# A two-layer convolution and low-rank kernel on one core: order and queues of the moved sample columns

## The reference, cut to what matters

```python
# layer 0: a grouped convolution over the 1024 columns, with a row of context per sample
h = conv1d(x, weight, groups=4, taps=9, pad=4) + ctx[:, :, None] + bias[None, :, None]
# then a dense layer 1024 -> 1024 with a rank-masked low-rank term (the rank chosen per row)
x = x + h @ W.T + b + sel(h @ A[:r].T @ B[:, :r].T)
# layer 1: a per-sample 64x64 channel mixture (weights from a small network), then a dense layer
# 1024 -> 1024 with a sparsemax-weighted mixture of 8 rank-16 experts
h = agg_w @ x + agg_b
x = x + h @ W_base.T + b_base + experts(h)
```

## Time and profile before

| | us |
|---|---|
| median of 3 runs | 519.87 |
| lowest, highest | 519.02, 521.14 |
| the profiled execution's own time | 518.63 |
| its span | 516.8 |
| PE busy | 497.5 (96%) |
| DVE busy | 364.4 (71%) |
| ACT busy | 152.4 (29%) |
| POOL busy | 167.9 (32%) |
| mean granted TensorE clock | 0.993 |

### The profile page before, as it was taken

One profiled execution on the slowest core, in us unless ns is written; L12 is line 12 of the kernel. 1 busy time (PEld: TensorE's weight loads), 2 busy tenths in 40 slices (PEclk: granted clock), 3 DMA queues, 4 the chain that ended last, 5 costly groups with the idle time before them and its releaser, 6 DMA issues.

```text
span 516.8 us, 8425 instructions
## 1 busy us (share of the span) xinstructions
PE 497.5 (96%) x2857; PEld 456.8 (88%) x2857; DVE 364.4 (71%) x797; ACT 152.4 (29%) x322; POOL 167.9 (32%) x140
## 2 busy tenths in 40 slices
PE   9999999999989989798898999999999999999997
PEld 8989999999879879688797988899898989989886
DVE  3956997567765877687669976775676857566654
ACT  4732335152424236133235312211211212121200
POOL 1000020042455256445604316161523416161530
PEclk9999999999989989999999999999999999999999
DMA  8844206348565764856899924241424233160312
GB/s 319 302 157 153 81 1 185 112 134 268 199 217 192 249 202 127 275 176 190 280 376 413 412 101 150 98 167 44 174 90 146 99 122 124 62 204 1 122 42 82
DMA packets 46182, 88.47 MB, mean 171 GB/s; under 512 B 4795, under 2 KB 21787, under 8 KB 46140
## 3 DMA queue, kind: packets, MB, share of 16 engines
q1 hardware_dynamic: 37084, 65.56, 38.3%
q10 hardware_dynamic: 9056, 22.38, 11.4%
HBM read 58.79 MB, written 24.97 MB: 162 GB/s over the span
## 4 chain that ended last, share of the span: by engine, by line
PE 62%; DVE 9%; POOL 9%; DMA 7%; issue 7%; SPq 5%; ACT 1%; DVEq 0%; POOLq 0%
PE b_p L1725 5%; DMA z_moved<-a_lo_place 5%; PE b_x L1745 4%; PE b_x L1744 4%; PE b_x L1742 4%; PE b_m L1673 3%; PE b_p L1726 3%; PE b_y L1745 3%; PE b_y L1742 3%; PE b_y L1744 3%; DMA wp_place<-in_wcat 2%; POOL mixed L645 2%; PE b_m L1701 2%; SPq L432 2%; DVE a_lo L1140 2%
## 5 line engine op out<-in xcount | busy, mean ns | idle before, releaser
L1725 PE MATMUL b_p<-wp,a_hi 128*128 128x464 f32 (+1 forms) x224 | 76.5, 391 | 8.6 <-DVE a_lo L1140 8.4
L722 ACT CAST a_hi<-mixed 128x512 fp32r<-128x512 f32 x63 | 37.7, 620 | 148.8 <-DVE mixed L1107 80.3
L654 POOL TENSOR_TENSOR xs<-xs,mixw_sb 128x512 f32<-128x512 f32 x28 | 38.6, 1390 | 122.9 <-DMA xs<-x_scratch 87.8
L1140 DVE TENSOR_TENSOR a_lo<-mixed,a_hi 128x512 fp32r<-128x512 f32 x63 | 54.5, 898 | 20.5 <-ACT a_hi L722 20.0
L1726 PE MATMUL b_p<-wp,a_lo 128*128 128x232 f32 (+1 forms) x224 | 61.5, 275 | 0.0
L1725 PEld LDWEIGHTS b_p<-wp,a_hi 128*128 128x128 f32 x224 | 43.6, 195 | 15.5 <-issue 9.4
L733 ACT CAST s_hi<-s_sums 128x512 fp32r<-128x512 f32 x56 | 34.7, 621 | 72.5 <-POOL s_sums L617 34.6
L1148 DVE TENSOR_TENSOR s_lo<-s_sums,s_hi 128x512 fp32r<-128x512 f32 x56 | 46.5, 881 | 7.6 <-POOL s_sums L622 7.4
L1301 DVE TENSOR_TENSOR xs<-b_x,xs 128x464 f32<-128x464 f32 (+2 forms) x52 | 33.3, 640 | 25.4 <-PE b_x L1785 15.6
L1742 PE MATMUL b_y<-wb_hi,s_hi 128*128 128x464 f32 (+2 forms) x112 | 42.2, 377 | 3.8 <-ACT a_lo_place L849 2.0
L1726 PEld LDWEIGHTS b_p<-wp,a_lo 128*128 128x128 f32 x224 | 44.4, 198 | 0.6
(11 more groups left out here) (308 smaller groups left out, 1313.3 us busy)
## 6 DMA issues: line engine op xcount, KB each, us to landing
blk<-x_scratch SPq DMA_DIRECT2D x16, 512.0 KB, 4.0
xs<-in_x SPq DMA_DIRECT2D x30, 256.0 KB, 3.3
x_scratch<-xs SPq DMA_DIRECT2D x30, 256.0 KB, 4.1
xs<-x_scratch SPq DMA_DIRECT2D x28, 256.0 KB, 3.0
out_dram<-xs SPq DMA_DIRECT2D x27, 256.0 KB, 2.2
w_raw<-in_wcat SPq DMA_DIRECT2D x8, 546.0 KB, 8.9
blk<-in_xwhole SPq DMA_DIRECT2D x8, 512.0 KB, 4.2
praw<-in_wcat ACTq DMA_DIRECT2D x8, 464.0 KB, 4.3
```

The lines of the kernel that those rows point to most:

```text
L654: pool.tensor_tensor(x_rows, x_rows, bbase[:, a:b], ALU.add).then_inc(x_biased[q], 1)
L722: act.copy(a_hi[:, op, :, :], mixed[:, op, :, :]).then_inc(ahi_done[op], 1)
L1140: dve.tensor_tensor(a_lo[:, op, :, :], mixed[:, op, :, :], hi(a_hi[:, op, :, :]), ALU.subtract).then_inc(alo_done[op], 1)
L1725: pe.matmul(both, x_hi, wp[:, k, :, 0:PLAIN[l]], start=(k == 0), stop=False, skip_group_check=True)
```

## The change

Six things are moved, no arithmetic is changed. `move_z` is split: SyncE keeps two of its four DMAs (one of 112 rows, one of 15), ScalarE issues the other two, right behind the `take_z` of the sample. SyncE moves (a,1) before the x and block loads and (b,1) before tile b+2's block load; its x loads of pair 7 come later, with two waits. GpSimd adds (a,0) and (a,1) before `prep`, (b,0) and (b,1) behind it. ScalarE loads the weight piece after the second `cast_x`, takes and moves (b,1) before any `prep_split`, and stores the piece after A22. VectorE's list is reordered: `prep_split` and `low_x` of the next pair's first tile come later, the results that free banks between them.

```diff
--- before.py
+++ after.py
@@ -428,9 +428,7 @@
                 if sample(T, n) > 1:
                     sp.wait_ge(z_added, sample(T, n) - 1)
                 sp.dma_start(dst[1:EDGE + 1, 0, :], src[0:EDGE, 1, :]).then_inc(z_landed[n], 16)
-                sp.dma_start(dst[0:EDGE, 1, :], src[1:EDGE + 1, 0, :]).then_inc(z_landed[n], 16)
                 sp.dma_start(dst[EDGE + 1:P, 0, :], src[EDGE:P - 1, 1, :]).then_inc(z_landed[n], 16)
-                sp.dma_start(dst[EDGE:P - 1, 1, :], src[EDGE + 1:P, 0, :]).then_inc(z_landed[n], 16)
 
             half = FR_TAPS + HALF_FRONT
             sp.dma_start(first_in[:, FR_TAPS:half], front[:, FR_TAPS:half]).then_inc(s_taps[0], 16)
@@ -506,20 +504,18 @@
                     sp.wait_ge(fin12, g)
                     store_x(1, g - 1)
                     move_z(a, 0)
+                    move_z(a, 1)
                     stored(3, g - 1)
                     stored(1, g - 1)
                     load_x(3, g)
                     load_x(1, g)
                     sp.wait_ge(mix_done, steps(a + 1))
                     load_blocks(a + 2)
-                    move_z(a, 1)
                     move_z(b, 0)
+                    move_z(b, 1)
                     sp.wait_ge(mix_done, steps(b + 1))
                     load_blocks(b + 2)
-                    move_z(b, 1)
                     if g == PAIRS - 2:
-                        load_x(3, g + 1)
-                        load_x(1, g + 1)
                         sp.wait_ge(agg_stored, 16)
                     load_agg(g + 2)
                     sp.wait_ge(sum_done, steps(b + 1))
@@ -527,6 +523,11 @@
                     sp.wait_ge(fin11, g + 1)
                     sp.wait_ge(finq[0], g + 1)
                     store_x(0, g)
+                    if g == PAIRS - 2:
+                        sp.wait_ge(took_u2, made(g))
+                        sp.wait_ge(took_p5, made(g))
+                        load_x(3, g + 1)
+                        load_x(1, g + 1)
                     sp.wait_ge(fin21, g + 1)
                     sp.wait_ge(finq[1], g + 1)
                     store_x(2, g)
@@ -666,12 +667,14 @@
             pool.wait_ge(aggb_stored, 16)
             pool.memset(z_moved[1][:, :, :], 0.0).then_inc(zeroed, 1)
             for g in range(FULL, LAST + 1):
+                if shifted(2 * g + 2):
+                    add_z(2 * g + 2, 0)
+                    add_z(2 * g + 2, 1)
                 if PREP_FIRST <= g <= PREP_LAST:
                     prep(g)
                 if shifted(2 * g + 2):
-                    for T in (2 * g + 2, 2 * g + 3):
-                        for n in range(2):
-                            add_z(T, n)
+                    add_z(2 * g + 3, 0)
+                    add_z(2 * g + 3, 1)
                 if g == PAIRS:
                     pool.wait_ge(s_bbase, 16)
                     pool.wait_ge(gated, 4 * (2 * g + 2))
@@ -848,39 +851,51 @@
                 dst = z_out[n].rearrange("p v (a c) -> p v a c", c=CH)[:, :, :, CH // 2 * gp:CH // 2 * (gp + 1)]
                 act.copy(dst, src).then_inc(z_taken, 1)
 
+            def move_z(T, n):
+
+                src, dst = z_out[n], z_moved[n]
+                act.wait_ge(z_taken, 2 * sample(T, n) + 2)
+                if sample(T, n) == 0:
+                    act.wait_ge(zeroed, 3)
+                if sample(T, n) > 1:
+                    act.wait_ge(z_added, sample(T, n) - 1)
+                act.dma_start(dst[0:EDGE, 1, :], src[1:EDGE + 1, 0, :]).then_inc(z_landed[n], 16)
+                act.dma_start(dst[EDGE:P - 1, 1, :], src[EDGE + 1:P, 0, :]).then_inc(z_landed[n], 16)
+
             def shift_pair(g):
 
                 a, b = 2 * g + 2, 2 * g + 3
                 split_s(S2, g)
                 split_s(S4, g)
-                prep_load(g)
                 take_z(a, 0, 0)
                 take_z(a, 0, 1)
+                move_z(a, 0)
                 cast_x(b, 0)
                 gate_exp(2 * g)
                 gate_exp(2 * g + 1)
                 take_z(a, 1, 0)
                 take_z(a, 1, 1)
+                move_z(a, 1)
                 cast_x(b, 1)
+                prep_load(g)
                 take_z(b, 0, 0)
                 take_z(b, 0, 1)
-                prep_split(0, g)
-                prep_split(1, g)
+                move_z(b, 0)
                 split_ut(2 * g)
                 split_ut(2 * g + 1)
+                split_a(A11, g + 1)
+                take_z(b, 1, 0)
+                take_z(b, 1, 1)
+                move_z(b, 1)
+                split_a(A12, g + 1)
+                for part in (0, 1, 3, 2):
+                    prep_split(part, g)
                 if shifted(a + 2):
                     cast_x(a + 2, 0)
-                take_z(b, 1, 0)
-                take_z(b, 1, 1)
-                prep_split(3, g)
-                prep_split(2, g)
-                split_a(A11, g + 1)
-                split_a(A12, g + 1)
-                if shifted(a + 2):
                     cast_x(a + 2, 1)
-                prep_store(g)
                 split_a(A21, g + 1)
                 split_a(A22, g + 1)
+                prep_store(g)
                 split_s(S1, g + 1)
                 split_s(S3, g + 1)
                 if g == PREP_LAST:
@@ -1494,30 +1509,31 @@
                 sum_shift(b, 0, 1)
                 split_ut(2 * g)
                 split_ut(2 * g + 1)
-                if shifted(a + 2):
-                    low_x(a + 2, 0)
                 sum_shift(b, 1, 0)
                 sum_shift(b, 1, 1)
-                for part in (0, 1, 3, 2):
-                    prep_split(part, g)
-                dve.wait_ge(p_done[P6], made(g))
-                take(b_x, 1, g, took_u2)
                 split_a(A11, g + 1)
-                split_a(A12, g + 1)
                 dve.wait_ge(c11_done, g + 1)
                 dve.wait_ge(took_p1, made(g))
                 take(b_z, 0, g, fin11, BANK)
+                split_a(A12, g + 1)
+                dve.wait_ge(p_done[P6], made(g))
+                take(b_x, 1, g, took_u2)
+                prep_split(0, g)
+                prep_split(1, g)
                 dve.wait_ge(p_done[P5], made(g))
                 take(b_y, 3, g, took_p5)
+                dve.wait_ge(c21_done, g + 1)
+                take(b_w, 2, g, took_w, BANK)
+                prep_split(3, g)
+                prep_split(2, g)
                 dve.wait_ge(fin11, g + 1)
                 take_plain(0, g)
-                dve.wait_ge(c21_done, g + 1)
-                take(b_w, 2, g, took_w, BANK)
-                if shifted(a + 2):
-                    low_x(a + 2, 1)
                 dve.wait_ge(p_done[P7], made(g))
                 dve.wait_ge(took_w, made(g))
                 take(b_x, 2, g, fin21)
+                if shifted(a + 2):
+                    low_x(a + 2, 0)
+                    low_x(a + 2, 1)
                 take_plain(1, g)
                 split_a(A21, g + 1)
                 split_a(A22, g + 1)
```

## The result

| | before | changed |
|---|---|---|
| median, us | 520.28 (4 runs beside it) | 534.06 (4 runs) |
| lowest to highest, us | 519.02 to 521.14 | 533.29 to 535.36 |
| span of the profiled execution, us | 516.8 | 531.9 |
| mean granted TensorE clock | 0.993 | 0.987 |

The changed kernel is slower: ratio 1.0278, 95% interval 1.0241 to 1.0315. The forecast of 516.9 us, its range and its sign were wrong.

A forecast was written before the change was run, and what follows sets the result against it. The VectorE-ScalarE ring was taken to stay the bound: terms summed from 34.84 to 33.8 us a turn, -4.2 us over four turns, 3 after pair 7, giving 516.9 us; 8-in-10 range 508.5 to 523.5.

The forecast's parts named there:

- -4.09: VectorE's idle time before the last splits, waiting for sample (b,1), goes: 4.09 us less per turn.
- -1.1: Two prep casts leave ScalarE's list before the low-rank casts, for which VectorE idles: 1.1 us less per turn.
- -0.86: low_x of the next pair no longer makes VectorE wait for its block: 0.86 us less per turn.
- -0.7: VectorE's s_lo shrinks as GpSimd's sums come earlier, low_x moves beside them: 0.7 us less per turn (0 to -1.3).
- issues on ScalarE: ScalarE's two DMA issues per sample block its next cast: +1.46, +1.2, +1.46, +1.3 us behind the four samples.
- the later load: Weight piece issued some 10 us later, landing 4.3 us after; VectorE's first prep_split needs its sums: +0.3 us (0 to 1.5).
- The wait for (b,1): Second plain part: PE's largest wait, 8.4 us in four pieces, comes from the late sample (b,1) and leaves.
- the ring: VectorE and ScalarE hand each other work; one turn, 34.84 us, was to become 33.8 and stay the bound.
- gave back 1.2: Pair 7: ScalarE stands some 2.7 us for the store before load_home, cutting the gain from 4.2 to 3 us.
- B: Rival: ScalarE's issues are hidden and cost nothing, PE is the bound; 11 us less, 509 us; chance 0.22.
- C: Rival: slower, two of ScalarE's small issues per pair take 1.8 us under backlog; 524.5 us; chance 0.18.
- D: Rival: no change, pair 7's load takes all the gain or issues are 0.3 us longer each; 519.5 us; chance 0.20.

The follow-up runs named there:

- e5_sync_early: Changed kernel with all four DMAs of a sample on SyncE and the weight piece loaded before the first take: 511.81 us.
- e1_load_early: Changed kernel with one thing undone, ScalarE loading the weight piece before the first take again: 525.25 us.
- e2_sync_all: Changed kernel with all four DMAs of a sample issued on SyncE, the weight piece still loaded late: 521.16 us.
- e3_before_half: Kernel before with two of each sample's four DMAs issued by ScalarE behind its takes, other engines' orders kept: 532.46 us.

## Why the prediction was wrong

The table of experiments splits the turn. The mean turn (shift step to shift step, pairs 3 to 6) is 34.22 us before, 31.66 in `e5_sync_early` (31.01, 32.69, 31.29), 34.95 in `e1_load_early` and 37.57 in the changed kernel:

| per turn, us | forecast | measured |
|---|---|---|
| waits and casts removed (-4.09, -1.1, -0.86, -0.7) | -6.75 | -2.56 (before to e5) |
| issues on ScalarE (1.46, 1.2, 1.46, 1.3) | +5.42 | +3.29 (e5 to e1) |
| the later load | +0.3 | +2.62 (e1 to changed) |
| sum | -1.03 | +3.35 |

- **The wait for (b,1)** leaves, as the prediction said: the wait at the second plain is in no list of PE's waits of the changed kernel.
- **ScalarE's issues block it.** That was right, and so were the four places where they would show (VectorE idle 2.75, 1.38, 2.81, 2.23 us in pair 3). The sum of the terms was too large by 2.1 us (by 1.8 if `e2_sync_all`, 33.93 us a turn, is set against the changed kernel). Without the issues the ring is no longer the only bound: in pairs 3 and 5 of `e5_sync_early` PE is busy for 29.5 of 30.4 us. That part of each issue falls into this slack is argued, not shown.
- **The first step that failed** is the term "prep now starts at the landing of its load ... +0.3 (0 to 1.5)". It named the risk (1.9 MB of loads that slow each other) and took the low end: it kept the landing of 4.3 us from before. In the changed kernel prep could start only 8.0 us after the first issue, in all four pairs. Its last sum ended 3.6 to 5.7 us later than in `e1_load_early`, and VectorE, which never waits for prep there, waited 1.9 us for it in each pair, with b_y's take behind. It measured 2.62 us a turn (2.27 between `e5_sync_early` and `e2_sync_all`), outside its own bounds, and 8.8 to 9.4 us in all. The term had the right path for the changed kernel and a wrong size; that with SyncE issuing alone the same load costs as much by delaying the moves of (a,1), it did not have. The slow prep_lo is no part of this price: the two ahead of b_y take 2.9 to 3.2 us in `e1_load_early` too, against 3.3.
- **The second** is the credit: "-4.09", "-1.1", "-0.86" and "-0.7" were summed as if VectorE would gain each in full, and even without the two costs the turn shrank by 2.56 us only. `e5_sync_early` shows two limits. In pairs 3 and 5 PE is busy nearly throughout, and the sum without the issues, 28.4 us, lies below these 30.4. In pairs 4 and 6 b_y's take stands behind the wait for prep and two prep_lo of 1.6 to 1.7 us each, where the changed order puts them beside GpSimd's adds. What share of the missing 4.2 us each has, no run splits.
- The three turns of the table are 10.1 us. The fourth, up to pair 7's second plain part, is about the same: that pair starts 5.1 us later against its shift step, less the wait of 1.72 us that is gone. The rest, some 2 us, lies in pair 7, where the forecast gave back 1.2: ScalarE stood 4.4 us (262.98 to 267.35) before `load_home`, not 2.7, and PE's wait for b_z grew from 1.7 to 3.6 us.
- **The rivals.** B (509 us) would have needed free issues, and `e3_before_half` excludes it. C (524.5 us) had the sign, by luck. Its mechanism, issues of 1.8 us under the backlog, is seen only in the longest rows (137.11 took 1.66 us, the medians of L863 are 0.87 and 0.90), and it is not the cause: the issues together cost less than forecast, and `e1_load_early` keeps all of them and is 8.8 us faster. D (519.5 us) had the turn as forecast, at 33.8 us, and it was 37.57.
- **The page.** The Trainium skill's page DMA: Bandwidth & Descriptors, section Issuing engines are not separate DMA queues, says that issuing from more engines saves no more than the sequencer's time. The trace agrees where the loads stand alike: with the piece early the median landing of a move is 2.5 us with the issues split (`e1_load_early`) and 2.7 with all on SyncE (`e5_sync_early`). With the piece late it is 2.7 (changed) and 4.0 (`e2_sync_all`), where the piece's load goes ahead of the moves of (a,1). That this time is "usually small relative to the DMA itself" doesn't hold for these copies: 1.46 us of issue per sample beside 2.7 us.

## What to carry to other kernels

A DMA issue that waits for the engine's own last result, as each move waits for its takes, holds that engine's in-order list for its full issue time; put it on a queue with nothing urgent behind it. (The piece's two issues at 129.12 wait for nothing and ran beside the cast at 129.10.) When a load is moved, ask in both directions what it then travels with: which transfers make it late, and which it makes late. Take the landing from a place with such company and not from the old place, and follow it to the first engine that stands idle for it. When two costs are suspected, build the two by two table: it showed here that they add, and it found the kernel that beats both. But equal prices in two cells are not yet one cause; each cell's trace has to say what came last.

## What was not expected of the hardware

- VectorE and GpSimd slow each other when both do elementwise work. prep_lo (128x464) takes 0.65 us in the kernel before (203.99), where it is nearly alone, and 1.6 us beside GpSimd's adds at 142.62. GpSimd's own operations there take 1.45 us each (142.47) and not 1.28 (130.63). VectorE's takes out of a bank are not slowed: that of b_y at 145.80, beside GpSimd's first sum S, takes 0.60 us, and the same shape takes 0.59 us in `e2_sync_all` at 129.16, where GpSimd is idle.
- The 15-row copies cost more to issue than the 112-row ones: medians 0.80 to 0.90 us against 0.54 to 0.57, on either queue.
- Two loads of 464 KB landed in 4.2 us (median) with the x and block loads 5 us away, and in 6.1 us when these started within about 1 us of them. The company works both ways: the 112-row moves of the second samples land in 3.9 us (median) in `e2_sync_all`, where the piece's load starts 0.3 us ahead of those of (a,1), and in 2.5 us in `e5_sync_early`.
